# A two-layer graph network on 32 pairs: the column split, the product W a and the order of work rewritten

## The chip, the cores and the metric

One core of a Trainium2 chip runs the whole program. The metric is the device time of one execution in microseconds (us), lower is better; the median of the runs is compared. TensorE is the matmul engine (PE in the profile), DVE is VectorE, ACT is ScalarE, POOL is GpSimd, SP is the engine whose queue issues the transfers. PSUM is the memory that TensorE writes, eight banks of 128x512 f32; SBUF is the one that all engines read.

## The reference, cut to what matters

The input x is 64 batch entries of 128 nodes with 256 features, adj a 128x128 matrix of zeros and ones. Two residual layers follow one another.

```python
h = relu(layernorm(x))
# layer 0: graph attention with 4 heads, then one with 1 head, then an FFN
Wh = einsum('bnf,hfo->bhno', h, W)
f1, f2 = Wh @ a[:, :O], Wh @ a[:, O:]                  # per node and head
e = leaky(f1[..., :, None] + f2[..., None, :], 0.01)
attn = softmax(where(adj > 0, e, -1e9))
h2 = elu(attn @ Wh)                                    # heads side by side: 1024 features
out = elu(attention(h2, W_out, a_out))                 # the same with one head, 256 features
x = x + layernorm(relu(out @ w1 + b1) @ w2 + b2 + out) * gamma + beta
# layer 1
h3 = relu(layernorm(x))
x = x + deg * (h3 @ Wi.T + b) + adj @ (h3 @ Wj.T)
```

## The kernel before

Two batch entries form a pair; 32 pairs run through a pipeline of 8 stages. `steps` (L255) unrolls 39 steps on each engine. In step t, `pairs[k]` is pair t - k, if it exists, and each engine's function `one` lists the operations of all stages in one order, written out by hand; the same order is used in every step, and an engine goes strictly through it. What an operation needs it waits for with `wait` on a semaphore counter in `S`; `wait_bank` on TensorE waits until the last reader of a PSUM bank is done (which operation that is follows from the order). `B_...` (L41 to L60) gives each product its bank.

Precision: a factor is split into a high part in f32r (a copy by ACT, `..._hi`) and a low part (a subtraction by DVE or POOL, `..._lo`), and `three` (L1203) makes three products of them.

The path of a pair, with the names in the code:
- `norm1_stats`, `rstd1`, `norm1`: layer norm of x. `h_transposes` (L1269) and `ht_copy` give h transposed.
- `score_cols` (L1279): f1 and f2 of both entries as 16 columns, from h transposed times `wa` = W a (128 x C x 2 x H). `wa` is made once: DVE takes 16 dot products of rows of W with rows of a (`heads_dots` L523), for which each row of a_heads is loaded 128 times over (`ah_bc`, L273).
- The 16 columns must become rows that hold f2 exactly in bf16. `f_cols` (L601) writes them three times, at columns 32, 64 and 96 of a 128x128 tile `f_rep`; `score_rows` (L1291) transposes it in f32; `f_first` on ACT (L990) casts the rows to bf16, the first part; `f_less_first`, `f_second`, `f_third` (L587 to L599, through `less_first`, `second`, `third`) leave on DVE the second part in partitions 64 and up and the third in 96 and up. `scores` (L1297) multiplies them by the selector `rowsel`, which adds the three parts and repeats the row.
- `score_mask` (L643) adds f1 and the mask; `score_leaky`, `soft_max`, `soft_exp`, `soft_sum`, `soft` give the probabilities, `prob_transposes` (L1311), `at_high`, `at_low` their transposes.
- `gh_unit` (L1209) times u = 0..3 is h times attention, `gh_high` and `gh_low` split it; `h2_unit` (L1227), eight per pair, multiplies by W; `elu_exp`, `elu_less` (POOL), `elu` (DVE), `h2_high`, `h2_low` (POOL) make h2; `wh2_part` (L1250), eight per pair, multiplies by W_out, with W_out a_out as two more columns.
- The second attention has the same split on its 4 columns: `wh2_scores` (L665, once per entry), `score_rows2` (L1322), `g_first` to `g_third` (L617 to L630, on DVE), `scores2` (L1328), then `score_mask2` to `soft2`, `prob_transposes2`, `a2_copy`, `out2` (L1344).
- `out_exp`, `out_less`, `out_elu`, `ov_high`, `ov_low`; `hidden`, `hidden_relu`, `hidden_whole`, `hidden_low`; `ffn_out`, `ffn`, `add_b2`; `norm2_*`, `rstd2`, `norm2`, `scale2`, `add_beta`, `residual2`.
- `norm3_*`, `rstd3`, `norm3`, `h3_transposes` (L1387), `h3t_high`, `h3t_low`, `mixed` (L1397), `mj_high`, `mj_low`, `add_mi`, `gather` (L1412), `result`, `store`.

The transfers are issued on SP: x of the pair, then once the four parts of W and of a (L270), then W_out, a_out and the last weights (L275), w1 and w2 when the dots are done (L280), and in each step the residual's x and the store. Four constant rows are loaded by POOL's queue (L334). `out_dots` (L530) makes W_out a_out on DVE.

TensorE's order in a step before: scores 0, prob_transposes2, wh2 (0,0), out2, gh 0, scores 1, wh2 (1,1), gh 1, mixed 1, wh2 (1,2), gh 2, wh2 (0,1) (0,2), h_transposes, gh 3, wh2 (0,3) (1,3), score_cols, gather, hidden 0 and 1, score_rows2, h2 (0,0) (0,1), ffn_out, h2 (1,0), scores2, h3_transposes, score_rows, h2 (1,1), ffn 0 and 1, h2 (2,0), prob_transposes 0, h2 (2,1) (3,0) (3,1), wh2 (1,0), mixed 0, prob_transposes 1.

Of the kernel before, what the change touches and what calls it, by code (L numbers as in the profile page):

```python
# [21 lines left out]
BF16 = mybir.dt.bfloat16  # L22
# [14 lines left out]
G3 = (32, 64, 96)  # L37
# [3 lines left out]
B_HT = 5  # L41
B_COLS = 5
B_ROWS = 5
B_SCORES = (5, 4)
B_PROBS = (6, 6)
# [3 lines left out]
B_ROWS2 = 7  # L49
B_SCORES2 = 6  # L50
B_PROBS2 = 7
B_OUT = 7
B_HIDDEN = 6
B_FFN = 7
B_H3T = 4
B_M = (4, 6)
B_LAST = 4
B_ADJ = 2
B_L1W = (2, 3)


class Pair:
# [8 lines left out]
    def exists(self):  # L71
        return not isinstance(self.i, int) or 0 <= 2 * self.i + self.c < PAIRS

# [10 lines left out]
def build(nc, x, adj, w_heads, a_heads, w_out, a_out, w1, b1, w2, b2, gamma, beta, l1w, l1b, out):  # L84
    ctx = ExitStack()
    with ctx:
# [17 lines left out]
        rowsel = sb("rowsel", [P, 4 * H, P], BF16)  # L104
        sel = sb("sel", [P, 4 * H])
# [21 lines left out]
        ah_bc = lend2[:, 0:2, :, :, :].rearrange("p x y h m -> p (x y) (h m)")  # L127
# [27 lines left out]
        f_rep = two("f_rep", [P, P])  # L155
        f_parts = same("f_parts", [P, P], BF16)
        f_rest = same("f_rest", [P, P])
# [8 lines left out]
        f2_rep = two("f2_rep", [P, P])  # L166
        g_parts = two("g_parts", [P, P], BF16)
        g_rest = two("g_rest", [P, P])
# [23 lines left out]
        out_in, ffn_in, last_in = sem("out_in"), sem("ffn_in"), sem("last_in")  # L192
        adj_in, consts_in, memset_done, ident_ready = sem("adj_in"), sem("consts_in"), sem("memset_done"), sem("ident_ready")
# [6 lines left out]
        dotted = sem("dotted")  # L200
        w_hi_ready, w_lo_ready = sem("w_hi_ready"), sem("w_lo_ready")
# [6 lines left out]
        for per, names in (  # L208
# [5 lines left out]
                "rows_third"),  # L214
# [7 lines left out]
            (2, "wh2_done wh2_copied wh2_scores_copied exps2_done"),  # L222
            (1, "rows2_done rows2_first rows2_rest rows2_second rows2_third scores2_done "
# [41 lines left out]
        DOTS_HEADS, DOTS_ALL = 2 * C * H, 2 * C * H + 2 * K2  # L265
# [3 lines left out]
        def _(sp):  # L269
            def load_heads():  # L270
                for hd in range(H):
                    sp.dma_start(wh[:, :, hd, :], w_heads[hd].rearrange("(c f) o -> f c o", f=P)).then_inc(heads_in[hd], 16)
                    sp.dma_start(ah_bc[:, hd, :], a_heads[hd].partition_broadcast(P)).then_inc(heads_in[hd], 16)  # L273

            def load_later_weights():  # L275
                sp.dma_start(wo[:, :, :], w_out.rearrange("(k f) o -> f k o", f=P)).then_inc(out_in, 16)
                sp.dma_start(ao_bc[:, :, :], a_out.rearrange("(j o) -> j o", j=2).partition_broadcast(P)).then_inc(out_in, 16)
                sp.dma_start(l1w_sb[:, :, :], l1w.rearrange("(k o) d -> o k d", o=P)).then_inc(last_in, 16)

            def load_ffn_weights():  # L280
                sp.wait_ge(dotted, DOTS_HEADS)
# [21 lines left out]
            def one(pairs):  # L303
# [8 lines left out]
                if p := pairs[6]:  # L312
                    store(p)
                if p := pairs[2]:
                    load_residual(p)
# [6 lines left out]
        def _(pool):  # L322
# [11 lines left out]
            for dst, src in ((b2_bc, b2), (gamma_bc, gamma), (beta_bc, beta), (l1b_bc, l1b)):  # L334
                pool.dma_start(dst[:, :], src.partition_broadcast(P)).then_inc(consts_in, 16)
# [56 lines left out]
            def scale2(p):  # L392

                if p.is_first():
                    pool.wait_ge(consts_in, 80)
# [11 lines left out]
            def add_beta(p):  # L407

                if p.is_first():
                    pool.wait_ge(consts_in, 80)  # L410
# [29 lines left out]
            def one(pairs):  # L440
                if p := pairs[5]:
                    out_less(p)
                if p := pairs[4]:
                    h2_low(p, 3)
                if p := pairs[6]:
                    scale2(p)
                if p := pairs[5]:
                    ov_low(p)
                if p := pairs[2]:
                    h_low(p)  # L450
                if (p := pairs[3]) and p.is_first():
                    out_low()
                if (p := pairs[4]) and p.is_first():
                    ffn_low()
                if p := pairs[5]:
                    add_beta(p)
                if p := pairs[6]:
                    rstd3(p)
                if p := pairs[5]:
                    hidden_low(p)  # L460
                if p := pairs[3]:
                    elu_less(p, 0)
                if p := pairs[2]:
                    soft(p, 0)
                if (p := pairs[3]) and p.is_first():
                    out_scores_low()
                if p := pairs[3]:
                    elu_less(p, 1)
                if p := pairs[6]:
                    add_bias(p)  # L470
                if p := pairs[3]:
                    h2_low(p, 0)
                if p := pairs[2]:
                    soft(p, 1)
                if p := pairs[3]:
                    elu_less(p, 2)
                    elu_less(p, 3)
                    h2_low(p, 1)
# [4 lines left out]
                if p := pairs[0]:  # L483
                    rstd1(p)
# [4 lines left out]
        def _(dve):  # L489
# [11 lines left out]
            dve.memset(f_rep[0][:, :], 0.0)  # L501
            dve.memset(f_rep[1][:, :], 0.0)
            dve.memset(f2_rep[0][:, :], 0.0)
            dve.memset(f2_rep[1][:, :], 0.0)

            def selectors():

                dve.wait_ge(ident_ready, 1)
                dve.tensor_tensor(sel[:, :], ident[:, G3[0]:G3[0] + 4 * H], ident[:, G3[1]:G3[1] + 4 * H], ALU.add).then_inc(sel_ready, 1)
                dve.wait_ge(sel_ready, 1)  # L510
                dve.tensor_tensor(sel[:, :], sel[:, :], ident[:, G3[2]:G3[2] + 4 * H], ALU.add).then_inc(sel_ready, 1)
# [11 lines left out]
            def heads_dots(hd):  # L523
# [995 lines left out]
```

## Time and profile before

| what | value |
|---|---|
| runs | 907.23, 907.75, 909.05 us; median 907.75 |
| the profiled execution | 909.05 us, span of its instructions 907.2 us |
| TensorE (PE) busy | 836.8 us, 92% of the span |
| weight loads (PEld) | 776.6 us, 86%, beside the products |
| DVE, ACT, POOL busy | 757.1 (83%), 683.0 (75%), 703.9 us (78%) |
| mean granted TensorE clock | 0.989 |
| DMA | 31.5 MB, mean 35 GB/s, 246 GB/s in the first of 40 slices |

The span runs from the first to the last instruction. Products of TensorE overlap, so the distance from the start of one to the start of the next says more than its duration. "ps<-gh_hi,wh_hi" reads: written tile, and the tiles read. A time in brackets behind a row of the timeline is the idle time of that engine before it, with what ended it. The trace knows tiles by their memory, so `lend`, `wo`, `l1w_sb` and `h_hi` also stand for the tiles that share it or look alike.

### The profile page before, as it was taken

Reading aid. Unit: us, or ns where it says so; the run is one execution under the profiler, and the core shown is the slowest. Engines: PE = TensorE matmul, PEld = TensorE weight load, DVE = VectorE, ACT = ScalarE, POOL = GpSimd, SP = SyncE. Lnnn points to the kernel's source line nnn. Section 1 sums busy time; section 2 is a strip of 40 time slices with the busy share of each in tenths; the row PEclk is TensorE's granted clock in tenths of the full one; section 3 lists DMA queues with packets and bytes.
Section 4 is the critical chain, followed back from the end, with each engine's and each line's share of the span. In section 5 each row is a group of like instructions: output and inputs, shape, how many; then the busy total and the mean of one; then the engine's idle time right before and its main releaser. Section 6 shows DMA issues by size and latency. Waiting matters only on the chain.

```text
span 907.2 us, 20067 instructions
## 1 busy us (share of the span) xinstructions
PE 836.8 (92%) x6281; PEld 776.6 (86%) x6281; DVE 757.1 (83%) x1998; ACT 683.0 (75%) x1801; POOL 703.9 (78%) x948
## 2 busy tenths in 40 slices
PE   2699999999999999999999999999999999999964
PEld 1589989889998988999898899889889998989952
DVE  4978888898888889888888988888899888897753
ACT  3788878787777878778787877778777877877541
POOL 3587988877788887778888777888877788888852
PEclk9999999999999999999999999999999999999987
DMA  8100010111111011111101111110111111000000
GB/s 246 59 1 24 25 36 2 36 36 36 35 37 35 1 36 36 36 36 36 34 4 36 36 36 36 36 35 3 35 37 36 36 37 35 2 24 25 25 24 23
DMA packets 30136, 31.50 MB, mean 35 GB/s; under 512 B 1856, under 2 KB 28992, under 8 KB 30032
## 3 DMA queue, kind: packets, MB, share of 16 engines
q1 hardware_dynamic: 29776, 29.63, 10.5%
q8 instruction: 52, 0.85, 0.4%
q0 software_dynamic: 256, 0.59, 0.3%
q14 instruction: 52, 0.43, 0.2%
HBM read 21.82 MB, written 8.39 MB: 33 GB/s over the span
## 4 chain that ended last, share of the span: by engine, by line
PE 66%; DVE 17%; issue 9%; POOL 3%; ACT 2%; DMA 1%; SPq 0%; DVEq 0%; POOLq 0%; ACTq 0%
PE ps L1201 59%; DVE g_parts L598 4%; PE ps L1319 3%; DVE wo L711 2%; DVE lend L737 2%; PE ps L1275 2%; PE ps L1393 2%; DVE mj_lo L768 1%; DMA lend<-in_L_gnn_a_heads 1%; ACT mj_hi L1086 1%; DVE c_st L568 1%; DVE g_rest L589 1%; DVE g_parts L621 1%; DVE f_rep L669 1%; PE ps L1341 1%
## 5 line engine op out<-in xcount | busy, mean ns | idle before, releaser
L363 POOL TENSOR_TENSOR h_lo<-h2v,h_hi 128x512 fp32r<-128x512 f32 x128 | 166.6, 1302 | 0.1
L1201 PE MATMUL ps<-gh_hi,wh_hi 128*128 128x256 f32 x512 | 153.7, 300 | 1.6 <-DVE h2v L641 1.1
L1201 PE MATMUL ps<-wo_hi,h_hi 128*128 128x258 f32 x512 | 150.6, 294 | 0.0
L1201 PE MATMUL ps<-wo_lo,h_hi 128*128 128x258 f32 x512 | 145.1, 283 | 0.0
L1201 PE MATMUL ps<-wo_hi,h_lo 128*128 128x258 f32 x512 | 145.0, 283 | 0.0
L1201 PE MATMUL ps<-gh_lo,wh_hi 128*128 128x256 f32 x512 | 142.9, 279 | 0.0
L1201 PE MATMUL ps<-gh_hi,wh_lo 128*128 128x256 f32 x512 | 142.7, 279 | 0.0
L369 POOL TENSOR_SCALAR h2e<-h2e 128x512 f32<-128x512 f32 x128 | 86.2, 681 | 32.0 <-ACT h2e L959 31.8
L1201 PEld LDWEIGHTS ps<-wo_lo,h_hi 128*128 128x128 f32 x512 | 97.4, 190 | 4.3
L1201 PEld LDWEIGHTS ps<-wo_hi,h_hi 128*128 128x128 f32 x512 | 96.8, 189 | 4.6 <-POOL h_lo L363 0.4
L970 ACT ACTIVATE lend<-lend,zm 128x128 f32<-128x128 f32 x256 | 99.1, 393 | 0.0
L1201 PEld LDWEIGHTS ps<-gh_hi,wh_hi 128*128 128x128 f32 x512 | 96.5, 188 | 2.1 <-DVE h2v L641 1.5
L641 DVE SCALAR_TENSOR_TENSOR h2v<-h2e,ps 128x512 f32<-128x512 f32 x128 | 87.5, 683 | 12.9 <-POOL h2e L369 6.4
L582 DVE TENSOR_TENSOR gh_lo<-ps,gh_hi 128x512 fp32r<-128x512 f32 x128 | 87.7, 686 | 11.9 <-ACT gh_hi L948 11.9
L404 POOL TENSOR_TENSOR lend<-lend,zr 128x512 f32<-128x512 f32 x64 | 69.5, 1087 | 35.9 <-DVE zr L663 35.9
L1201 PEld LDWEIGHTS ps<-wo_hi,h_lo 128*128 128x128 f32 x512 | 97.0, 189 | 0.0
L1201 PEld LDWEIGHTS ps<-gh_hi,wh_lo 128*128 128x128 f32 x512 | 96.8, 189 | 0.0
L1201 PEld LDWEIGHTS ps<-gh_lo,wh_hi 128*128 128x128 f32 x512 | 96.7, 189 | 0.0
L948 ACT ACTIVATE gh_hi<-ps 128x512 fp32r<-128x512 f32 x128 | 75.8, 592 | 10.8 <-PE ps L1201 7.5
L1005 ACT ACTIVATE h_hi<-h2v 128x512 fp32r<-128x512 f32 x128 | 80.5, 629 | 0.3 <-DVE h2v L641 0.2
L959 ACT ACTIVATE h2e<-ps 128x512 f32<-128x512 f32 x128 | 72.1, 588 | 2.0 <-PE ps L1201 1.4
L413 POOL TENSOR_TENSOR wo<-xr,beta_bc 128x512 f32<-128x512 f32 x32 | 41.3, 1291 | 40.7 <-DVE lend L737 40.7
(166 smaller groups left out, 2794.3 us busy)
## 6 DMA issues: line engine op xcount, KB each, us to landing
xa<-in_x SPq DMA_DIRECT2D x32, 256.0 KB, 3.1
xr<-in_x SPq DMA_DIRECT2D x32, 256.0 KB, 3.0
out<-res SPq DMA_DIRECT2D x32, 256.0 KB, 2.2
lend<-in_L_gnn_W_heads SPq DMA_DIRECT2D x4, 256.0 KB, 5.7
lend<-in_L_gnn_a_heads SPq DMA_DIRECT2D x4, 256.0 KB, 8.4
wo<-in_L_gnn_W_out SPq DMA_DIRECT2D x1, 1024.0 KB, 11.2
l1w_sb<-in_L_gnn_W SPq DMA_DIRECT2D x1, 512.0 KB, 9.7
lend<-in_L_gnn_w SPq DMA_DIRECT2D x2, 256.0 KB, 3.0
```

The costliest lines, as they stand in the source:

```text
L363: pool.tensor_tensor(h2_lo[:, u, :, :].rearrange("p c n -> p (c n)"), h2v[u % 2][:, :], h2_hi[:, u, :, :].rearrange("p c n -> p (c n)").bi ...
L369: pool.tensor_scalar(h2e[u % 2][:, :], h2e[u % 2][:, :], 1.0, -1.0, ALU.mult, ALU.add).then_inc(S["heads_less"], 1)
L404: pool.tensor_tensor(zn[:, b, :, :], zp[:, b, :, :], zr[p.e][:, b, :].unsqueeze(2).broadcast_to([P, H, P]), ALU.mult).then_inc(S["probs_re ...
L413: pool.tensor_tensor(xb, xr[p.e][:, :, :], beta_bc[:, :].unsqueeze(1).broadcast_to([P, 2, F]), ALU.add).then_inc(S["x_plus_beta"], 1)
L582: dve.tensor_tensor(gh_lo[:, c, :, b, :], ps[:, B_GH[u], :].rearrange("p (h n) -> p h n", h=H), gh_hi[:, c, :, b, :].bitcast(F32), ALU.sub ...
L598: dve.tensor_tensor(parts[p.e][96:P, :], rest[p.e][96:P, :], parts[p.e][96:P, :], ALU.subtract)\
L641: dve.scalar_tensor_tensor(h2v[i][:, :], h2e[i][:, :], 0.0, ps[:, B_H2[u], :], ALU.min, ALU.max).then_inc(S["heads_elu"], 1)
L948: act.activation(gh_hi[:, c, :, b, :], ps[:, B_GH[u], :].rearrange("p (h n) -> p h n", h=H), ACT.Copy).then_inc(S["gh_hi"], 1)
L959: act.activation(h2e[u % 2][:, :], ps[:, B_H2[u], :], ACT.Exp).then_inc(S["heads_exp"], 1)
L970: act.activation(zp[:, b, hd, :], zt[:, b, hd, :], ACT.Exp, bias=zm[p.e][:, b, hd:hd + 1], accum_out=zs[p.e][:, b, hd:hd + 1]).then_inc(S[ ...
L1005: act.activation(h2_hi[:, u, :, :].rearrange("p c n -> p (c n)"), h2v[u % 2][:, :], ACT.Copy).then_inc(S["heads_hi"], 1)
L1201: return pe.matmul(out_, lhs, rhs, start=start, stop=stop)
```

## The change

**The split on columns.** The columns are split before they are turned into rows. `split_cols` on DVE copies the columns out of PSUM as f32 (for score_mask), casts them to bf16 as first part, subtracts that in PSUM itself, casts the rest as second part, and subtracts to the third. The three parts stand side by side at columns 0, 16 and 32 of a zeroed bf16 tile of 128x128 (`f_split`, `g_split`), which `score_rows` multiplies by the bf16 identity; one copy brings the rows to SBUF (ACT for f, DVE for g). `wh2_scores` now handles both entries at once.

**W a by TensorE.** The rows of a come as one 16x128 tile, are transposed once, each head's W is transposed by four transposes, copied by DVE, and multiplied in `heads_products`; the steps of these stand between the parts of pairs 0 and 1 in TensorE's order. The loads of a_heads for all partitions are gone. The four constant rows are loaded by SP, behind a_out and before the last weights.

**Identity products.** `warm(n, bank)` issues n products of the bf16 identity with itself, 128x512, into a bank that is not in use: 6 before the transposes of W, 2, 10, 3, 2 and 6 around the score steps of pairs 0 and 1, and at the end 10 before hidden of pair 31, 6 before h3_transposes of pair 30, 3 before its gather, and for pair 31 15, 4 and 3 before h3_transposes, mixed and gather.

**The orders** of all four engines, the banks and the wait_bank lists are new; store and load_residual change places on SP, and the stages are counted otherwise (store is in stage 7, load_residual in 3).

```diff
+            def split_cols(name, p, cols, whole, parts):
+                dve.tensor_copy(whole, cols).then_inc(S[name[0]], 1)
+                dve.tensor_copy(parts[0], cols).then_inc(S[name[1] + "_first"], 1)
+                wait(dve, name[0], p)
+                wait(dve, name[1] + "_first", p)
+                dve.tensor_tensor(cols, cols, parts[0], ALU.subtract).then_inc(S[name[1] + "_rest"], 1)
+                wait(dve, name[1] + "_rest", p)
+                dve.tensor_copy(parts[1], cols).then_inc(S[name[1] + "_second"], 1)
+                wait(dve, name[1] + "_second", p)
+                dve.tensor_tensor(parts[2], cols, parts[1], ALU.subtract).then_inc(S[name[1] + "_third"], 1)
...
             def score_rows(p):
-                wait(pe, "cols_copied", p)
-                pe.transpose(ps[:, B_ROWS, 0:P], f_rep[p.e][:, :], ident[:, :]).then_inc(S["rows_done"], 1)
+                wait(pe, "rows_third", p)
+                mm(ps[:, B_ROWS, 0:P], f_split[p.e][:, :], ident_bf[:, :], True, True).then_inc(S["rows_done"], 1)
...
+            def heads_transposes(hd):
+                pe.wait_ge(heads_in[hd], 16)
+                if hd >= 2:
+                    pe.wait_ge(wh_t_copied, hd - 1)
+                for k in range(C):
+                    for c in range(C):
+                        last = pe.transpose(ps[:, B_WHT[hd % 2], k * F + c * P:k * F + (c + 1) * P],
+                                            wh[:, c, hd, k * P:(k + 1) * P], ident[:, :])
+                last.then_inc(wh_t_done, 1)
+            def heads_products(hd):
+                pe.wait_ge(wh_t_copied, hd + 1)
+                pe.wait_ge(a_cols_ready, 1)
+                for c in range(C):
+                    for k in range(C):
+                        last = mm(ps[:, B_WA, 0:COLS].rearrange("p (c j h) -> p c j h", c=C, j=2)[:, c, :, hd],
+                                  wh_t[:, hd % 2, k * F + c * P:k * F + (c + 1) * P], a_cols[:, hd, :, k], k == 0, k == C - 1)
+                last.then_inc(wa_done, 1)
+            def warm(n, bank):
+                for _ in range(n):
+                    pe.matmul(ps[:, bank, :].rearrange("p (k n) -> p k n", k=4), ident_bf[:, :], ident_bf[:, :].unsqueeze(1).broadcast_to([P, 4, P]),
+                              start=True, stop=True)
```

TensorE's order in a step after (once-only parts in brackets): wh2 (1,2) (1,3), h2 (0,0) (0,1), [products 2], h2 (1,0), [products 3], h2 (1,1), score_cols, prob_transposes 0, hidden 0 and 1, score_rows2, h2 (2,0), score_rows, [a_transpose], scores2, [transposes 0 and 1], h2 (2,1) (3,0), ffn_out, [products 0], scores 0, h3_transposes, [transposes 2], h2 (3,1), wh2 (0,0), ffn 0 and 1, gh 0, mixed 0, [adj_transpose], prob_transposes2, mixed 1, wh2 (1,0), prob_transposes 1, out2, wh2 (0,1), [l1w_transposes], scores 1, gh 1, h_transposes, [transposes 3], wh2 (0,2), gather, [products 1], gh 2, wh2 (1,1), gh 3, wh2 (0,3).

DVE after: soft_max 1, norm3_stats, norm1, norm3_var, wh2_scores, elu 0, f_cols_split, rows2_copy, elu 1, soft_sum 1, hidden_whole, score_mask2, at_low 0, soft_max2, elu 2, h3t_low, soft_sum2, soft2, score_mask 0, add_b2, norm2, elu 3, add_mi 0, gh_low 0, mj_low 0 and 1, add_mi 1, soft_max 0, at_low 1, gh_low 1, score_mask 1, soft_sum 0, out_elu, gh_low 2, result, gh_low 3, residual2.

ACT after: wh2_copy 0 and 1, elu_exp 0, soft_exp 1, elu_exp 1, h2_high 0, hidden_relu, at_high 0, rows_copy, norm3, elu_exp 2, score_leaky2, h3t_high, [out_scores_high], h2_high 1, soft_exp2, elu_exp 3, [out_high], norm1, mj_high 0, a2_copy, h_high, h2_high 2, gh_high 0, score_leaky 0, mj_high 1, at_high 1, h2_high 3, out_exp, gh_high 1, soft_exp 0, gh_high 2, norm2, gh_high 3, score_leaky 1, ht_copy, ov_high.

POOL after: add_beta, elu_less 0, rstd1, elu_less 1, rstd3, h2_low 0, hidden_low, elu_less 2, h2_low 1, soft 1, elu_less 3, add_bias, [out_low], rstd2, h2_low 2 and 3, out_less, h_low, soft 0, scale2, ov_low.

## Rows read from the trace of the kernel before

**Rows 1.** Busy time of each engine in one steady period; columns: PE, PEld, DVE, ACT, POOL.
```profile
450.05:476.50 26.45, 25.58 (x198) 23.95 (x197) 23.22 (x61) 20.95 (x58) 21.56 (x29) 1.00 0.10 31
```

**Rows 2.** Waits: who waited for whom; total us, times, longest.
```profile
PE ps L1201 <- DVE g_parts L598: 25.4, 29, 1.2
```

**Rows 3.** Timeline of a steady period; start us, us, engine, line.
```profile
504.15 1.27 POOL L390 TENSOR_TENSOR hid_lo<-wo,hid_hi 128x512 fp32r<-128x512 f32 x1 [0.93 <-DVE wo L711]
504.22 1.36 DVE L598 TENSOR_TENSOR g_parts<-g_rest,g_parts 32x128 bf16<-32x128 f32 x1
...
504.49 0.28 PE L1201 MATMUL ps<-gh_hi,wh_lo 128*128 128x256 f32 x1
...
505.63 0.29 PE L1201 MATMUL ps<-g_parts,rowsel 128*128 128x128 bf16 x2 [0.87 <-DVE g_parts L598]
```

**Rows 4.** Groups of DVE instructions by line and form; busy us, mean ns.
```profile
L598 DVE TENSOR_TENSOR g_parts<-g_rest,g_parts 32x128 bf16<-32x128 f32 x32 | 39.2, 1224 | 1.0
...
L594 DVE CAST f_parts<-f_rest 64x128 bf16<-64x128 f32 x32 | 26.3, 822 | 1.0
...
L669 DVE COPY f_rep<-ps 128x6 f32<-128x6 f32 x64 | 9.8, 153 | 0.5 <-ACT l1w_sb L976 0.3
...
L598 DVE TENSOR_TENSOR f_parts<-f_rest,f_parts 32x128 bf16<-32x128 f32 x32 | 9.2, 289 | 1.0
...
L594 DVE CAST g_parts<-g_rest 64x128 bf16<-64x128 f32 x32 | 7.2, 224 | 1.1
```

**Rows 5.** Timeline of TensorE in stretches without a wait.
```profile
51.51 0.39 PE L1201 MATMUL ps<-f_parts,rowsel 128*128 128x128 bf16 x4
51.71 0.37 PE L1201 MATMUL ps<-wo_hi,h_hi 128*128 128x258 f32 x1
51.91 0.29 PE L1201 MATMUL ps<-wo_lo,h_hi 128*128 128x258 f32 x1
52.03 0.29 PE L1201 MATMUL ps<-wo_hi,h_lo 128*128 128x258 f32 x1
...
827.75 0.39 PE L1201 MATMUL ps<-l1w_hi,h_hi 128*128 128x512 f32 x1
827.98 0.40 PE L1201 MATMUL ps<-l1w_lo,h_hi 128*128 128x512 f32 x1
```

**Rows 6.** Groups by line and form on ACT and DVE, for the prices of chains.
```profile
L948 ACT ACTIVATE gh_hi<-ps 128x512 fp32r<-128x512 f32 x128 | 75.8, 592 | 10.8 <-PE ps L1201 7.5
...
L981 ACT ACTIVATE lend<-wo,b_nm,b_rs 128x256 f32<-128x256 f32 x64 | 34.6, 590 | 1.4 <-POOL b_nm L358 1.4
...
L582 DVE TENSOR_TENSOR gh_lo<-ps,gh_hi 128x512 fp32r<-128x512 f32 x128 | 87.7, 686 | 11.9 <-ACT gh_hi L948 11.9
```

**Rows 7.** The start: one row of the DMA issues, then the timeline.
```profile
lend<-in_L_gnn_W_heads SPq DMA_DIRECT2D x4, 256.0 KB, 5.7
...
14.24 0.42 DVE L499 SCALAR_TENSOR_TENSOR res<-lend 128x256 f32<-128x256 f32 x1 [2.88 <-DMA lend<-in_L_gnn_a_heads]
...
17.37 1.88 PE L1201 MATMUL ps<-wa,ht 128*128 128x8 f32 x8 [4.36 <-DVE res L499]
...
24.18 1.11 PE L1275 MATMUL ps<-ident,h 128*128 128x128 f32 x4 [1.75 <-ACT h L981]
...
40.20 0.66 PE L1275 MATMUL ps<-ident,h 128*128 128x128 f32 x4 [0.40 <-ACT h L981]
...
43.27 0.36 PE L1201 MATMUL ps<-gh_hi,wh_hi 128*128 128x256 f32 x1 [0.46 <-DVE gh_lo L582]
```

**Rows 8.** The end: timeline of TensorE; the first row is the last wh2 product.
```profile
859.82 0.28 PE L1201 MATMUL ps<-wo_hi,h_lo 128*128 128x258 f32 x1
...
894.19 1.11 PE L1393 MATMUL ps<-ident,lend 128*128 128x128 f32 x4 [3.89 <-ACT lend L981]
...
899.93 0.63 PE L1201 MATMUL ps<-l1w_lo,h_hi 128*128 128x512 f32 x1
900.36 0.63 PE L1201 MATMUL ps<-l1w_hi,h_lo 128*128 128x512 f32 x1
```

More of the change, by code:

```diff
@@ L441, in one @@
                 if p := pairs[5]:
[L442 to L455, printed above, removed]
-                    add_beta(p)
+                    add_beta(p)
+                if p := pairs[3]:
+                    elu_less(p, 0)
+                if p := pairs[0]:
+                    rstd1(p)
+                if p := pairs[3]:
+                    elu_less(p, 1)
                 if p := pairs[6]:
                     rstd3(p)
+                if p := pairs[3]:
+                    h2_low(p, 0)
                 if p := pairs[5]:
@@ L461, in one @@
                 if p := pairs[3]:
[L462 to L472, printed above, removed]
+                    elu_less(p, 2)
+                    h2_low(p, 1)
                 if p := pairs[2]:
@@ L482, in one @@
                     h2_low(p, 2)
-                if p := pairs[0]:
-                    rstd1(p)
+                    h2_low(p, 3)
+                if p := pairs[4]:
+                    out_less(p)
+                if p := pairs[1]:
+                    h_low(p)
+                    soft(p, 0)
+                if p := pairs[5]:
+                    scale2(p)
+                if (p := pairs[4]) and p.is_first():
+                    ffn_low()
+                if p := pairs[4]:
+                    ov_low(p)
             steps(one)
@@ L614, in f_third, with wh2_scores @@
-            def f_third(p):
-                third("rows", p, f_parts, f_rest)
-            def g_first(p):
+                split_cols(("cols_copied", "rows"), p, ps[:, B_COLS, 0:COLS], f_cols[p.e][:, :],
+                           [f_split[p.e][:, k * COLS:(k + 1) * COLS] for k in range(3)])
+            def wh2_scores(p):
+                wait(dve, "wh2_copied", p)
+                wait(dve, "rows2_done", p, lag=1)
+                split_cols(("wh2_scores_copied", "rows2"), p, ps[:, B_WH2[0]:B_WH2[0] + 2, F:WO], g_cols[p.e][:, :, :],
+                           [g_split[p.e][:, k * COLS:k * COLS + 4].rearrange("p (b j) -> p b j", b=2) for k in range(3)])
@@ new lines, in one @@
+                if p := pairs[2]:
+                    score_cols(p)
+                if p := pairs[3]:
+                    prob_transposes(p, 0)
+                if (p := pairs[6]) and p.number() == 31:
+                    warm(10, 0)
+                if p := pairs[6]:
+                    hidden(p, 0)
+                    hidden(p, 1)
+                if p := pairs[5]:
+                    score_rows2(p)
+                if p := pairs[4]:
+                    h2_unit(p, 2, 0)
+                if (p := pairs[2]) and p.number() == 0:
+                    warm(3, 0)
@@ L1482, in one @@
                 if p := pairs[4]:
+                    h2_unit(p, 3, 1)
+                    wh2_part(p, 0, 0)
+                if p := pairs[6]:
                     ffn(p, 0)
                     ffn(p, 1)
+                if p := pairs[3]:
+                    gh_unit(p, 0)
+                if (p := pairs[7]) and p.number() == 31:
+                    warm(4, 0)
+                if p := pairs[7]:
+                    mixed(p, 0)
+                if (p := pairs[1]) and p.is_first():
+                    adj_transpose()
```

669 lines of the change are left out of this document (337 added, 332 removed).

## The prediction

> **What bounds the kernel now.** I read the busy shares by engine first (the table above: TensorE 92%, more than any other), then one period of the steady part, then who waited for whom, and the two ends last. A pair of batch entries passes every 26.45 us; in such a period TensorE works 25.58 us, and DVE, ACT and POOL 23.2, 21.0 and 21.6 [rows 1]. So TensorE is the bound and idles 0.87 us per period. One wait makes up that idleness: 25.4 us in 29 times, always before the products that read g_parts [rows 2]. The timeline of one period shows how: the third part of the split (L598) starts at 504.22, just after POOL's subtraction L390 at 504.15, and lasts 1.36 us; TensorE's last product before it starts at 504.49, the next at 505.63 [rows 3]. The same line on f_parts takes 289 ns, on g_parts 1224 ns; L594 is 224 ns on g_parts and 822 on f_parts [rows 4]. The long ones end when a POOL instruction ends: two engines in each other's way. The Trainium skill (SBUF — State Buffer, Who interferes with whom) says that a DVE instruction with two SBUF inputs waits for a GpSimd instruction that reads SBUF, and that a PSUM input lifts this; the trace's 1224 ns agree. By it the changed split can't be held up, since none of its operations has two SBUF inputs.
>
> **Part 1, the split on columns.** Removed per pair: three small widening copies (two of them 153 ns), two subtractions, and the casts and third parts, 1224 + 289 + 822 + 224 ns [rows 4]: over 2.9 us of DVE. Added: two splits of five dependent operations on 128x16 and 128x4, and one copy of 128x128 on DVE that was there before under another name (g_first). The nearest row is the copy of 128x6 out of PSUM at 153 ns; with a hop to the next I take 5 x 0.18 = 0.9 us each. Upper end: one of the five is held by POOL as L598 was, 1.36 us, then 2.1; lower end 0.8. DVE loses about 1 us of work per period and is not the bound; ACT's copy of the rows stays as it was. On TensorE two f32 transposes of 128 columns (one start each 0.11 us) become bf16 products (0.05 each by the four in 0.20 us of [rows 5]); but behind those four the second product comes 0.20 us after the first and not 0.12, so I set the exchange at nothing, from -0.1 to +0.1 us per pair.
> What goes is the wait: **25.4 us**, unless another replaces it.
>
> **Part 2, the new orders.** The work on TensorE stays at 25.58 us per period, so I laid its new order out by starts of 0.12 us for 256 columns and 0.23 for 512 [rows 5]: six products 0.70, mixed 1.40, gh_unit 0.71, transposes of four 0.44, score_cols and out2 0.9 each. From the start of a period: score_cols ends at 5.2, rows2 is at 7.1, score_rows at 7.9, scores2 at 8.0, h3_transposes at 10.3, gh_unit 3 ends at 24.9. Then the chains that must fit:
> f_cols_split has from 5.4 to 7.9, needs 0.9, and DVE first ends elu 0 at 6.4: slack 0.6, gone if one of the five is held for 1.36.
> rows2_copy (about 0.29) has from 7.45 to 8.0: slack 0.25. Behind scores2 on TensorE everything would wait.
> elu 1 stands behind rows2_copy on DVE and ends at 8.45, its bank is wanted at 8.8: 0.3.
> h3_transposes wait for norm3 (1.1 us on ACT), which waits for rstd3 on POOL, behind ov_low, add_beta, two elu_less and rstd1. I get h3 ready at 10.15 against 10.3: slack 0.1.
> h2_unit 0 waits for the last gh_low. Between gh_unit 3 and it stood 4.4 us of products (two wh2 parts, score_cols, gather, hidden, rows2); now three wh2 parts, 2.16. Needed are 0.3 to end, 0.59 and 0.69 on ACT and DVE [rows 6], hops 0.15: 1.7. On ACT norm2 (two of 590 ns, [rows 6]) stands ahead of gh_high 3, so slack is 0.2.
> Four slacks under 0.3 us with steps known to 0.05: I take 0.1 us of new waiting per period, 3 us in 30, bounds 0 and 0.4 (12 us). Store and residual load change places on SP's queue; they carry 256 KB per pair that land in about 3 us, hidden. POOL loses four DMA issues at the start, where it waits anyway.
>
> **Part 3, the start.** The products of W a now wait for the broadcast rows of a: DVE's dots stood 2.88 us for them, and score_cols of pair 0 began at 17.37 [rows 7]. After: four loads of W alone. Issued from 1.7 at 0.45 us each, with half the bytes in the way, they should have landed by 9 (the median of W was 5.7 us from issue [rows 7]). TensorE then does four transposes and four f32 products per head: at 1.11 us per four transposes and 1.88 us per four f32 products, which the trace counts as eight [rows 7], 4 x 3.0 = 12 us. Its clock: four transposes took 1.11 us at 24.18 and 0.66 us at 40.20 [rows 7], so it ran at 1.2 GHz at the first and at 2.4 at the second, whatever the granted clock prints there; at 2.4 GHz the 12 us are some 6.5. Now TensorE works from about 3 us on (six products of the identity first). If it is at 2.4 GHz from about 11 us, W a is done at 14 and score_cols ends at 16, not at 19.3: 3.3 us gained. If it stays at 1.2 GHz, W a is done at 18.5 and score_cols at 21.5, 2.2 lost. From there the first h2_unit (43.27 [rows 7]) took 24 us, with out_dots on DVE in the middle. After, out_high, norm1 and h_high stand ahead of score_leaky on ACT and out_dots still ahead of the maximum, but scores waits for nothing else, and both soft steps come before out_low on POOL; the same walk gives 21. So h2 starts at 37 (fast clock) to 42 (slow); I take 38.5, gain 4.8. Of that 1.0 is not gained, as score_cols of pair 2 now comes after it. l1w is issued behind four more broadcasts, some 3 us later; TensorE waits for it with scores(0,1) and h_transposes(1) queued behind. Those are wanted about 5 us after scores(0,0), so that is hidden up to about 23 us.
>
> **Part 4, the end.** From the last wh2 product (its slot ends at 859.94) to 907.2 there are 47.3 us [rows 8]. Products at 1.2 GHz lie in it: in the last mixed ten of twelve start 0.43 us apart [rows 8] against 0.23: 2.0 us. The last h3_transposes take 1.11 [rows 8] against 0.66: 0.45. By the same ratio twelve products of the last ffn and eight of the last hidden lose 0.1 each, 2.0, and the gather before it 0.3. In all 4.7 at best. Also out2 should come about 0.8 earlier. The identity products fill gaps: 15 before the last h3_transposes take 3.5 us at 0.23 each in a gap of 3.9 [rows 8]; at 1.2 GHz they take 6.5 and delay it by 2.6. I take 4.5 of a possible 5.5, lower end 1.
> The Trainium skill (TensorE: Matmul & The Clock Gate, Part 4) states that transposes don't count as activity for the clock. The rows can't show it: no stretch has transposes alone. By it the start's 16 transposes would not help the clock, h2 would start at 42 and the sum would be 3.5 us higher; rival (b) has that case with a chance of its own.
>
> **The sum.** The profiled execution took 909.05 us, its span 907.2; the median of the runs is 907.75, 1.3 below. 909.05 - 25.4 + 3 - 4.8 + 1.0 - 4.5 = 878.35; against the median 877.
>
> **Rivals.** (a) A new wait takes the place of the old: at h3_transposes, scores2 or h2_unit 0, of 0.3 to 0.9 us per period. For it: slacks of 0.1 to 0.25. Against: back-to-back ACT steps overlap by about 0.1 us, which I left out. At 0.45 us: 877 - 3 + 13.5 = 887.5; at 0.9, 901. Chance 0.17.
> (b) The identity products don't lift the clock, so the change doesn't do what it says: the start at 42 (3.5 lost), the end gains 1 (3.5 lost): 884. For it: at the start transposes and waits surround them. Chance 0.15.
> (c) Slower: h2_unit 0 waits for gh_low 3, whose chain has lost 2.2 us of cover. If soft_exp and norm2 on ACT are late, everything behind h2_unit 0 moves, every period. It decides from about 1.1 us per period (32 us in 30); 2 us of lateness would give, less the 0.5 of cover, 1.5 x 30 = 45: 877 - 3 + 45 = 919. Against: ACT works 21.0 of 25.6 us. Chance 0.07.
> (d) The forecast: 868 to 884, chance 0.61.
>
> **The numbers.** Down to 867: no new wait (3), start at 37 (1.5), the end at its best (1.0), products shorter by 0.1 us per period (3) and a rest of 1.5 for idle spots that I left standing. Up to 889: (b), and (a) up to 0.5 us. A measurement of this kernel tells 0.2% from no change. Faster 0.91 (d, a, b, less what (a) leaves near none), same 0.02, slower 0.07.
>
> **What would show it.** Right: the period falls to 25.5 to 25.8 us; no DVE step of the two splits is over 0.3 us; the first wh_hi product of pair 0 starts before 41 us; the products of the last mixed start 0.23 us apart. Wrong: a line of TensorE in the waits with about 30 entries and over 6 us, above all behind gh_low, h3 or the g_parts copy; TensorE work per period far from 25.6.

## The result and the profile after

The kernel after takes 871.21 us (median of 4 runs, 869.2 to 872.8) against 908.16 for the kernel before beside it: a ratio of 0.9592, 95% interval 0.9567 to 0.9617. The forecast was 877, the range 867 to 889. The profiled execution took 870.21 us with a span of 868.3; against 907.2 that is 38.9 us to account for.

The page's busy shares:

```profile
PE 849.3 (98%) x6400; PEld 785.6 (90%) x6400; DVE 701.7 (81%) x2002; ACT 668.0 (77%) x1801; POOL 693.6 (80%) x944
```

One period of the steady part, start to start of the products that read g_parts, answers to [rows 1] (columns: busy us of PE, PEld, DVE, ACT, POOL, then the granted clock, DMA share, GB/s):

```profile
460.03:485.41 25.38, 25.38 (x198) 23.97 (x198) 21.30 (x62) 20.48 (x57) 21.32 (x30) 1.00 0.10 28
```

TensorE is busy in every one of the 25.38 us. The period was 26.45, so it fell by 1.07, and only 0.87 of that was idle time: the busy time for the same number of TensorE instructions (198) also fell by 0.20 us, from the 25.58 of before. Half of that belongs to the wait too, as rest_psum shows below. These are all the waits of TensorE of at least 0.5 us in total (total us, times, longest), to be read against [rows 2]:

```profile
PE ps L1414 <- ACT lend L968: 3.3, 2, 2.3
PE ps L1210 <- POOL ident_bf L343: 2.8, 1, 2.8
PE ps L1222 <- ACT ht L974: 2.5, 1, 2.5
PE ps L1222 <- DVE gh_lo L601: 1.6, 1, 1.6
PE ps L1222 <- POOL ov_lo L397: 1.5, 2, 1.3
PE ps L1414 <- DVE l1w_sb L675: 1.1, 1, 1.1
PE ps L1222 <- ACT f_parts L980: 0.8, 2, 0.5
PE ps L1222 <- DVE h_lo L759: 0.5, 1, 0.5
PE ps L1222 <- DVE mj_lo L765: 0.5, 2, 0.3
PE ps L1222 <- DVE g_parts L635: 0.5, 1, 0.5
```

None comes more than twice: all lie at the two ends, the one behind g_parts too (at 828.98). Nothing took the place of the 29 waits behind g_parts. The groups of the split on DVE (busy us, mean ns), against [rows 4]:

```profile
L612 DVE TENSOR_TENSOR ps<-ps,f_split 128x16 f32<-128x16 f32 x32 | 5.9, 183 | 3.3
L614 DVE CAST f_split<-ps 128x16 bf16<-128x16 f32 x32 | 5.6, 174 | 1.1
L616 DVE TENSOR_TENSOR f_split<-ps,f_split 128x16 bf16<-128x16 f32 x32 | 5.6, 174 | 1.1
```

and one of them in full (ns min/median/max, first and last start us):

```profile
L612 DVE TENSOR_TENSOR ps<-ps,f_split x32: 182/183/183, 17.8 to 762.5; 128x16 f32<-128x16 f32 x32
```

No step was ever held: 182 to 183 ns over all 32 pairs, where L598 had a mean of 1224.

The start and the end on TensorE's timeline, against [rows 7, 8]; the first row is the first product of wh_hi of pair 0 (43.27 before), the others belong to the end:

```profile
40.27 0.36 PE L1222 MATMUL ps<-gh_hi,wh_hi 128*128 128x256 f32 x1 [1.63 <-DVE gh_lo L601]
...
852.52 3.41 PE L1210 MATMUL ps<-ident_bf 128*128 128x512 bf16 x15
858.19 0.66 PE L1414 MATMUL ps<-ident,lend 128*128 128x128 f32 x4 [2.26 <-ACT lend L968]
...
860.60 0.40 PE L1222 MATMUL ps<-l1w_lo,h_hi 128*128 128x512 f32 x1
860.83 0.39 PE L1222 MATMUL ps<-l1w_hi,h_lo 128*128 128x512 f32 x1
```

The last four transposes take 0.66 us in place of 1.11, the last products start 0.23 us apart in place of 0.43, and the fifteen products of the identity end 2.26 us ahead of the next real work, so they delay none. With the last wh2 product at 826.31 (its slot of 0.12 us ends at 826.43), the account of the 38.9 us is:

| stretch | before, us | after, us | gain |
|---|---|---|---|
| span's start to the first wh_hi product of pair 0 | 43.27 | 40.27 | 3.0 |
| from there to the end of the last wh2 product | 816.67 | 786.16 | 30.5 |
| from there to the end of the span | 47.3 | 41.9 | 5.4 |

### The profile page after: what moved, and what is told of

Read it like the earlier page. It is cut to its first block, busy times and chain, and to the rows that moved or that the text cites. A ratio compares the mean times of both kernels' runs of the same rounds, so it can differ in the third digit from the quotient of the medians.

```text
span 868.3 us, 20346 instructions
## 1 busy us (share of the span) xinstructions
PE 849.3 (98%) x6400; PEld 785.6 (90%) x6400; DVE 701.7 (81%) x2002; ACT 668.0 (77%) x1801; POOL 693.6 (80%) x944
## 4 chain that ended last, share of the span: by engine, by line
PE 94%; POOL 2%; DVE 1%; ACT 1%; issue 1%; POOLq 0%; ACTq 0%; DVEq 0%
PE ps L1222 84%; PE ps L1340 4%; PE ps L1414 2%; PE ps L1296 2%; PE ps L1395 2%; PE ps L1362 1%; PE ps L1210 1%; ACT lend L968 0%; ACT lend L957 0%; PE ps L1181 0%; DVE res L510 0%; POOL wo L425 0%; POOL lend L409 0%; POOL h_lo L375 0%; DVE lend L734 0%
## 5 line engine op out<-in xcount | busy, mean ns | idle before, releaser
L946 ACT ACTIVATE h2e<-ps 128x512 f32<-128x512 f32 x128 | 75.6, 591 | 32.7 <-PE ps L1222 32.7
L416 POOL TENSOR_TENSOR lend<-lend,zr 128x512 f32<-128x512 f32 x64 | 71.8, 1123 | 23.9 <-DVE zr L668 23.9
L381 POOL TENSOR_SCALAR h2e<-h2e 128x512 f32<-128x512 f32 x128 | 79.8, 623 | 10.1 <-ACT h2e L946 9.9
L656 DVE SCALAR_TENSOR_TENSOR lend<-ps,f_cols,mask_bf 128x128 f32<-128x128 f32 x256 | 71.4, 339 | 0.8 <-PE ps L1222 0.8
```

The costliest lines, as they stand in the source:

```text
L381: pool.tensor_scalar(h2e[u % 2][:, :], h2e[u % 2][:, :], 1.0, -1.0, ALU.mult, ALU.add).then_inc(S["heads_less"], 1)
L416: pool.tensor_tensor(zn[:, b, :, :], zp[:, b, :, :], zr[p.e][:, b, :].unsqueeze(2).broadcast_to([P, H, P]), ALU.mult).then_inc(S["probs_re ...
L656: last = dve.scalar_tensor_tensor(zt[:, b, hd, :], ps[:, B_SCORES[b], hd * P:(hd + 1) * P], f_cols[p.e][:, f1:f1 + 1], mask_bf[:, :], ALU. ...
L946: act.activation(h2e[u % 2][:, :], ps[:, B_H2[u], :], ACT.Exp).then_inc(S["heads_exp"], 1)
```

## The experiments

Twelve runs followed in three lots, each beside runs of the kernel before. All medians in one place; the period is the median one of the profiled execution, where before has 26.45, and the last column is that of the same single execution:

| run | us, median | ratio to before, 95% | period, us | first wh_hi product, us |
|---|---|---|---|---|
| rest_psum | 882.47 | 0.9714 (0.9692 to 0.9736) | 25.48 | 43.40 |
| third_up | 884.52 | 0.9733 (0.9719 to 0.9748) | 25.52 | 43.07 |
| split_only | 898.10 | 0.9879 (0.9861 to 0.9898) | 25.92 | 42.00 |
| no_warm | 878.66 | 0.9666 (0.9652 to 0.9680) | 25.38 | 43.91 |
| rest_sbuf | 874.06 | 0.9623 (0.9607 to 0.9638) | 25.37 | 39.73 |
| dots_back | 867.81 | 0.9553 (0.9539 to 0.9568) | 25.22 | 42.93 |
| warm_end | 874.34 | 0.9622 (0.9609 to 0.9635) | 25.38 | 43.58 |
| late_dots | 874.91 | 0.9637 (0.9616 to 0.9658) | 25.38 | 41.03 |
| after_again | 871.10 | 0.9584 (0.9565 to 0.9602) | 25.38 | 41.91 |
| placed | 867.44 | 0.9541 (0.9519 to 0.9564) | 25.22 | 43.77 |
| pad64 | 871.91 | 0.9585 (0.9570 to 0.9601) | 25.38 | 42.20 |
| early_start | 871.62 | 0.9586 (0.9563 to 0.9608) | 25.22 | 42.83 |

### Is it the collision? rest_psum and third_up

Both start from the kernel before and keep its split of 128 columns. The first puts the rests in PSUM:

```diff
-dve.tensor_tensor(rest[p.e][64:P, :], psum[64:P, :], parts[p.e][64:P, :], ALU.subtract)
+dve.tensor_tensor(rest[64:P, :], psum[64:P, :], parts[p.e][64:P, :], ALU.subtract)
-g_parts, g_rest)
+g_parts, ps[:, B_WH2[0], 384:512])
```

> The kernel before with the rests of both splits written to PSUM and not to SBUF, nothing moved and nothing else changed, so that the second and third part read at most one operand from SBUF. Theory (DVE and POOL are in each other's way at SBUF): the third part of g falls from 1224 to about 290 ns, the cast of f from 822 to about 230, TensorE's 25.4 us of waiting behind g_parts go, the period is 25.6 us, the time about 908 - 25 = 883. Rival (the third part is late because DVE comes to it late): its duration falls little or the wait stays, the time is over 900.

The second moves one call:

```diff
 g_less_first(p)
 g_second(p)
+g_third(p)
...
-if p := pairs[5]:
-    g_third(p)
```

> The kernel before with the third part of g moved up on DVE, right behind the second part; operands stay in SBUF. In the trace POOL is idle there (about 502.96 to 504.15 of the steady period). Theory: the third part takes 290 ns there, the wait goes, time about 883, so that the stall was a matter of place too; the cast of f keeps its 822 ns. Rival: the port is held at any place, or hidden_whole now comes later and POOL's hidden_low with it: 890 or more.

In rest_psum the same two lines (groups on DVE, mean ns) are no longer held:

```profile
L598 DVE TENSOR_TENSOR g_parts<-ps,g_parts 32x128 bf16<-32x128 f32 x32 | 9.5, 297 | 1.0
L594 DVE CAST f_parts<-ps 64x128 bf16<-64x128 f32 x32 | 9.4, 294 | 1.0
```

The same run shows that the wait cost more than its idle time. In [rows 3] the product at 504.49 is followed by the one on g_parts at 505.63, 1.14 us later; here it is 0.16:

```profile
464.24 0.28 PE L1201 MATMUL ps<-gh_hi,wh_lo 128*128 128x256 f32 x1
464.40 0.29 PE L1201 MATMUL ps<-g_parts,rowsel 128*128 128x128 bf16 x2
```

So the wait took 0.98 us of a period and showed 0.87 as idle: a product of 0.28 us is overlapped by the next one where nothing waits, and that overlap was lost as well. With the instructions, orders and tiles of before but without the wait, the period is 25.48, not 25.58.

In third_up the operands stay in SBUF, the third part merely begins before GpSimd's subtraction hid_lo (at 463.50 in a steady period, hid_lo at 464.77):

```profile
L594 DVE CAST f_parts<-f_rest 64x128 bf16<-64x128 f32 x32 | 21.2, 662 | 1.0
L598 DVE TENSOR_TENSOR g_parts<-g_rest,g_parts 32x128 bf16<-32x128 f32 x32 | 9.2, 289 | 1.1
```

Either takes the 25.4 us of waiting away (1.1 us in two waits are left in rest_psum) and with it 24 to 26 us of the time. So the wait was the collision at one place of the period; two thirds of the whole gain needs neither the column split nor the new orders, and one moved line is enough for it. The cast on f_parts, still held at 662 ns in third_up, costs nothing in the middle, since no engine waits for it there. That cast has one SBUF input: the prediction had named two inputs only. The Trainium skill (SBUF — State Buffer, Who interferes with whom) lists copies and casts, where their operands meet its conditions, among what can take the pair of ports shared with GpSimd. The trace agrees: 822 and 662 ns on average from SBUF against 294 from PSUM.

### The column split without the new orders: split_only

The kernel before with `split_cols` in place of the old split, put where the copies f_cols and wh2_scores stood, all other orders as they were.

> The kernel before with the column split alone (both splits, bf16 products for the rows), in the old orders, without W a by TensorE and without identity products. Theory: the wait of 25.4 us goes, and TensorE's work per period falls by up to 0.2 us if the f32 transposes were dearer than the bf16 products: 877 to 883. Rival: the five dependent steps of g hold up score_rows2 in the old order by about 0.3 us per period: 890.

The wait behind g_parts is gone, yet 10.5 of 37 us is all it brings. The waits show what came instead:

```profile
PE ps L1355 <- ACT lend L944: 12.2, 32, 3.9
```

h3_transposes now wait for norm3 in every pair, and the period is 25.92. Half of the 12.2 us are the last three pairs (0.6, 1.5 and 3.9); in the middle it is 0.22 us in each. There too a wait costs more than its idle time: from the start of the product before to the start of the first transpose it is 0.43 us, where it is 0.06 in the kernel before. These 0.37 are most of the 0.44 by which the period is above that of rest_psum. Neither expectation had the place right: score_rows2 does not wait, h3_transposes do. That place is one of the prediction's rival (a), and in these orders it is real. So the column split needs the new orders, which keep h3 in time: the wait is absent from the middle after. The split was not needed for the gain in the middle, though: rest_psum had most of it in the old orders, and no_warm below, with the column split, the new orders and W a on TensorE, is 3.8 us faster than rest_psum.

### What the identity products are worth: no_warm and warm_end

no_warm issues none; warm_end keeps those of pairs 30 and 31 at the end.

```diff
-for _ in range(n):
+for _ in range(0):
     pe.matmul(ps[:, bank, :]...
```

> The changed kernel without any of the identity products, all else the same. Theory: steady part unchanged (period 25.4), products at 1.2 GHz come back at the end as before (some 4 us) and the start is 0 to 3 us later: 875 to 878 against 871. Rival: the identity products gain nothing, since they stand in waits that others end: 871 within 1 us.

> The kernel after with the identity products at the end alone (the 27 at the start left out). They fill gaps, so they are worth time by the clock alone. If the 7.5 us that all of them were worth is 3.6 at the start and 3.8 at the end, as the two profiles put it, this is 874.5 to 875.5 us with the first product of wh_hi at 43.5 to 44 and 41.9 us from the last product of wh2 to the end. If the start's products are worth nothing because a later wait absorbs the start, it is 871 to 872 us.

Without them the time is 878.66, with the end's alone 874.34, with all 871.1: 4.3 us at the end, 3.2 at the start; the runs with and without do not overlap in either case. They only fill idle time, so this is the clock's part. In no_warm the end shows it in the waits: what was 3.3 us behind lend is 7.5.

```profile
PE ps L1414 <- ACT lend L968: 7.5, 2, 5.7
```

That run also answers another question: W a on TensorE without them starts the first wh_hi product at 43.91, no earlier than the 43.27 of before, in one profile of each.

### Does W a belong on TensorE? dots_back

W a by sixteen dot products of VectorE again, a_heads loaded as broadcasts, everything else as after.

> The kernel after, with W a made by sixteen dot products of VectorE again (the vector a loaded as four broadcasts), identity products kept where they are. If W a on TensorE is worth time, the first product of wh_hi of pair 0 starts later than 40.3 by the 3 us or more that the dot products stand on VectorE ahead of score_cols of pair 0: 43 or later, 874 to 877 us. If W a on TensorE brings nothing by itself (the run without identity products had its first such product at 43.9, later than the 43.3 of the kernel before), it starts at 40 to 41 and the time is 870 to 872 us. Nothing after the first product of wh_hi changes: period 25.4, end 41.9 us after the last product of wh2.

The first wh_hi product moved back to 42.93, as the first theory had it, and yet the time fell, to 867.81. The steady period fell as well, to 25.22 us, although its instructions are those of the kernel after. Groups of TensorE by form over the same 500 us, first after, then dots_back (mean ns in the last column but one):

```profile
L1222 PE MATMUL ps<-gh_hi,wh_lo 128*128 128x256 f32 x320 | 90.2, 282 | 0.0
...
L1222 PE MATMUL ps<-w_hi,hid_hi 128*128 128x256 f32 x80 | 22.5, 281 | 0.0
```

```profile
L1179 PE MATMUL ps<-gh_hi,wh_lo 128*128 128x256 f32 x320 | 89.4, 279 | 0.0
...
L1179 PE MATMUL ps<-w_hi,hid_hi 128*128 128x256 f32 x80 | 22.1, 276 | 0.0
```

Three ns less for the one kind of product and five for the other; not every kind changed. What differs beside the start is where the tiles lie: a_rows and a_cols take 576 bytes of each partition, and all tiles allocated behind them lie that much higher.

### The place of the tiles: placed, pad64, after_again

```diff
-a_rows = sb("a_rows", [COLS, P])
-a_cols = sb("a_cols", [P, H, 2, C])
...
 res = two("res", [P, 2, F])
+a_rows = sb("a_rows", [COLS, P])
+a_cols = sb("a_cols", [P, H, 2, C])
```

pad64 adds 64 bytes in the old place; after_again is the kernel after.

> The kernel after, unchanged, so that it is timed on the same chip as the three beside it. The first four runs of it had a median of 871.2 us (869.2 to 872.8); 870 to 872 us is expected, with a period of 25.38 us.

> The kernel after with the two tiles that the change adds for a_heads (a_rows, a_cols: 576 bytes of each partition) allocated behind all the others, so that every later tile lies 576 bytes lower, where it lay in the run dots_back. Not one instruction differs. In dots_back the period of a pair was 25.22 us against 25.38 in the kernel after, and the products of gh with wh_lo took 279 ns on average against 282, those of w_hi with hid 276 against 281. If the place of the tiles is the cause, the period is 25.22 here too, the first product of wh_hi stays at 40.3, and the time is 4 to 5 us shorter than after_again (0.16 us by some 29 periods): 866 to 867 us. If the cause is something else that dots_back left out, nothing changes: within 0.5 us of after_again.

> The run placed with 64 bytes of padding where the two tiles were: every later tile lies 64 bytes higher than in placed and 512 bytes lower than in the kernel after. If only the address within 512 bytes matters, the period is that of the kernel after, 25.38 us, and the time that of after_again within 0.5 us. If nothing of the place matters, all three are equal. If the place matters in some other way, the period lies at neither 25.22 nor 25.38.

The copies of g_parts on DVE mark the period; in placed:

```profile
460.53 0.29 DVE L635 CAST g_parts<-ps 128x128 bf16<-128x128 f32 x1 [0.79 <-PE ps L1222]
485.75 0.29 DVE L635 CAST g_parts<-ps 128x128 bf16<-128x128 f32 x1 [0.79 <-PE ps L1222]
```

and in pad64:

```profile
461.32 0.29 DVE L636 CAST g_parts<-ps 128x128 bf16<-128x128 f32 x1 [0.81 <-PE ps L1223]
486.70 0.29 DVE L636 CAST g_parts<-ps 128x128 bf16<-128x128 f32 x1 [0.81 <-PE ps L1223]
```

25.22 against 25.38, and 867.44 against 871.91 us. Between these two the means of some products differ (gh_hi with wh_hi 295 against 298 ns, w_hi with hid_hi 276 against 281), those of others hardly do (wo_hi with h_hi 293 against 294), and one goes the other way (mj_lo with adj_t 398 against 392). Shown: not one instruction differs between placed and the kernel after, 64 bytes of shift bring the longer period back, and 512 bytes between pad64 and the kernel after do nothing. From the first wh_hi product to the end of the last wh2 product it is 786.16 us in both profiles of the kernel after and 781.6 in placed. So placed, which has a shorter median than both kernels, is the version to keep. Which operand's address matters, and why, these runs do not tell.

dots_back has the tiles where placed has them and takes 867.81 against 867.44. So W a on TensorE is worth nothing that can be measured here, though the two were timed in different lots.

### How much cover the split has: rest_sbuf

```diff
-dve.tensor_tensor(cols, cols, parts[0], ALU.subtract)
+dve.tensor_tensor(rest, whole, parts[0], ALU.subtract)
```

with the rests in SBUF tiles of 16 and 4 columns.

> The kernel after, except that the rests of both splits go to small SBUF tiles of 16 and 4 columns again, so that two of the five steps read two SBUF inputs beside GpSimd's work. If it is the collision with GpSimd on SBUF that made a step long, some steps of this split show a mean of 250 to 500 ns in place of 164 to 183 ns. If the period was freed by the shorter steps (168 ns each, whatever holds them), the time becomes more than 1% longer (over 880 us). My theory is that the columns' split stands so far ahead of its reader in the new orders that a held step is covered: 871 to 874 us, period 25.4 to 25.5, no wait of TensorE behind g_split or f_split of over 0.3 us on average.

```profile
L613 DVE TENSOR_TENSOR f_rest<-f_cols,f_split 128x16 f32<-128x16 f32 x32 | 16.2, 506 | 3.3
L613 DVE TENSOR_TENSOR g_rest<-g_cols,g_split 128x4 f32<-128x4 f32 x32 | 15.1, 472 | 3.3
```

The collision is back: 506 ns for 16 columns and 472 for 4, against 183 and 171. The period stays, at 25.37: in the middle the new orders cover the held steps. The time is 3 us longer all the same. It goes where the pipeline fills (from the first wh_hi product to the end of the last wh2 product the profile has 3.3 us more than that of the kernel after); the row product of f_split is late there:

```profile
64.92 0.22 PE L1223 MATMUL ps<-ident_bf,f_split 128*128 128x128 bf16 x1 [1.30 <-DVE f_split L617]
```

with another 1.4 us behind the same line between 38 and 60 us. My theory had the period right and the total too low.

### Two tries at the start: late_dots and early_start

late_dots moves the dot products of W_out behind others on VectorE, with group 3 ahead of gh_low 2 and 3 of pair 0, and GpSimd's wo_lo ahead of h_low(0). early_start is placed, with group 2 behind score_mask(0,1) and group 3 ahead of gh_low 0.

> The kernel after with the eight dot products that stand on VectorE between score_mask(0,0) and soft_max(0,0) moved into its later gaps, and GpSimd's low part of W_out moved from 32.6 to before h_low(0) (20.9 to 25.1). In the profile of the kernel after they hold soft_max(0,0) until 24.82 while its input is there by 22.9. If that chain sets the start, the first product of wh_hi of pair 0 starts 1.5 to 2.5 us earlier (38 to 39 against 40.27) and the time is 869 to 870 us. If the start is set by other waits (GpSimd's h_low, the clock at 1.2 GHz from 28 to 35), it starts at 39.8 or later and the time stays within 0.5 us of 871.2.

> The run placed with another order at the start: of the dot products for W_out, group 2 moves from ahead of soft_max(0,0) to behind score_mask(0,1), group 3 to ahead of gh_low 0 of pair 0; GpSimd's low part of W_out moves ahead of h_low(0). In late_dots the same idea brought the last gh product of pair 0 from 38.6 to 37.4, but group 3 then stood ahead of gh_low 3, TensorE waited 3.54 us for it and ran at 1.2 GHz afterwards. Here no dots stand there. My theory: first product of wh_hi of pair 0 at 37.5 to 39, clock at 2.4 GHz behind it, 1.5 to 2.5 us below placed: 864 to 865.5 us. If the start is given back later (the fill is bound by another engine), it equals placed within 0.5 us; if a held dot product or the clock takes it, it is slower than placed.

Both fell. In late_dots the gh products ended at 37.4, as hoped, but group 3 held gh_low:

```profile
41.03 0.36 PE L1222 MATMUL ps<-gh_hi,wh_hi 128*128 128x256 f32 x1 [3.54 <-DVE gh_lo L601]
...
42.76 0.42 PE L1222 MATMUL ps<-gh_lo,wh_hi 128*128 128x256 f32 x1
42.98 0.42 PE L1222 MATMUL ps<-gh_hi,wh_lo 128*128 128x256 f32 x1
```

and behind that wait products start 0.22 us apart in place of 0.12: the lower clock. The profiled execution is 2.3 us longer than that of after_again: it starts 0.9 earlier, loses 1.6 in the middle and 1.6 at the end, and the last is not explained. In early_start one dot product of the four beside GpSimd's subtraction was held until that subtraction had ended (ns min/median/max, then GpSimd's own):

```profile
L510 DVE SCALAR_TENSOR_TENSOR res<-wo,oe x4: 415/944/4390, 19.8 to 25.9; 128x256 f32<-128x256 f32 x4
```

```profile
L353 POOL TENSOR_TENSOR wo_lo<-wo,wo_hi x1: 4466/4466/4466, 19.8 to 19.8; 128x2048 fp32r<-128x2048 f32 x1
```

That put soft_max(0,0) 7.5 us behind the start of score_mask(0,0) (26.20 against 18.74), where placed has 4.9. By the medians early_start is 4.2 us slower than placed. That the held dot product took these 4.2 us is likely but not shown: the profiled executions are the fastest of the one (869.1) and the slowest of the other (870.0), and in them the first wh_hi product comes at 42.83 and 43.77. Whether the dots alone, moved without GpSimd's low part, gain anything wasn't tried.

## Why the prediction was right, and where it was off

The main mechanism held: the 25.4 us of waiting went whole, by the step named, and the five steps of a split take 0.95 us (f) and 0.90 us (g) from the first start to the last end, where 0.9 was taken. The forecast was 6 us too high against the median. By its own steps, the profiled execution being 8.1 us below the sum of 878.35:

- **New waits, taken as 3 us, were 0.** The wait list after has no line in the middle. The four slacks of 0.1 to 0.3 us all held. The range held it as its lower bound. That the danger was real split_only shows: the wait of h3_transposes cost 0.37 us there in each pair.
- **Work of TensorE per period, taken as unchanged at 25.58 us, was 25.38.** Over some 30 periods that is 6 us, twice the "3" that the range allowed for. Half of it is a mis-sized wait: the prediction took the idle time of 0.87 us as all that the wait behind g_parts cost, while by starts it cost 0.98, so that without it the same work takes 25.48 (rest_psum). For the other half, the prediction treated the cadence of a product as a property of its shape. The runs show it also hangs on where the tiles lie: 0.16 us per period for 64 bytes. How much of the remaining 0.10 is place, how much the two f32 transposes turned into bf16 products, and how much the new neighbours of each product (those of mj_hi with adj_t fell from 480 to 395 ns, those of ov_hi with w_hi rose from 282 to 301) isn't settled.
- **Middle as a whole:** 25.4 + 6 - 1.0 for score_cols of pair 2 = 30.4, against 30.5 in the table.
- **Start, taken as 4.8 (first wh_hi product at 38.5), was 3.0 in the first profile and 1.4 in the second** (41.91). Of the same kernel, then, one start differs from another by 1.6 us, and placed, with the same instructions, has 43.77. The durations show where: eight transposes of W and the last 24 small products of W a took 1.07 and 3.91 us in the one and 1.95 and 5.12 in the other,

```profile
8.76 1.07 PE L1181 MATMUL ps<-ident,lend 128*128 128x128 f32 x8
9.66 3.91 PE L1222 MATMUL ps<-a_cols,lend 128*128 128x2 f32 x24
```

```profile
9.68 1.95 PE L1181 MATMUL ps<-ident,lend 128*128 128x128 f32 x8
11.42 5.12 PE L1222 MATMUL ps<-a_cols,lend 128*128 128x2 f32 x24
```

  so TensorE reached 2.4 GHz before them in the first only. Of the seven profiles that have both W a on TensorE and its identity products, these transposes took 1.07 to 1.40 us in four and 1.95 in three; without the identity products of the start (no_warm, warm_end) 1.95 in both. The step that failed is "at 2.4 GHz from about 11 us": even in the first profile, where W a was done at 13.4 (forecast: 14), it fell back to 1.2 GHz (a granted clock of 0.50 from 12 to 20 us), and score_cols of pair 0 took 1.85 us as before and that of pair 1 1.74 after another gap, where 0.95 is the price at 2.4 GHz (43.19 in the first profile). Score_cols of pair 0 ended at 17.2 in place of 16, and from there to the first wh_hi product it took 23.0 us where the walk had 21. The gain that the start does have comes from the identity products (3.2 us), not from W a on TensorE (nothing measurable).
- **End, taken as 4.5, was 5.4**; 5.5 had been put as the most possible. 4.3 of it is the identity products', by no_warm and warm_end.

Sum of the errors against the profiled execution: 3 + 6 - 1.8 + 0.9 = 8.1. The errors of the two unpriced terms have one sign, those of the ends nearly cancel.

Rival (a) did not come about in the new orders and did in the old ones. Rival (b) fell: 7.5 us are the identity products'. The sentence of the Trainium skill (TensorE: Matmul & The Clock Gate, Part 4) that transposes don't count for the clock was not put to a test of its own by any of the runs. Rival (c) fell: the only wait behind gh_low is the 1.6 us of pair 0.

Of "what would show it": the split's steps below 0.3 us, the first product before 41 (in one profile of two) and the 0.23 us at the end came true; the period came out at 25.38, below the 25.5 to 25.8 given.

## What to carry to other kernels

When one wait repeats once per period, look first at the instruction that it ends on: if its mean is several times that of the same line on other data, another engine may hold it, and moving that one call or its operand out of SBUF may give most of what a rewrite gives. Price a wait by the distance between the starts of the two products around it, not by the idle time alone. When the engine that sets the bound no longer waits, its time per period still isn't fixed: allocate tiles that are used once behind those of the loop, and compare the period of two placements before trusting a difference of half a per cent. Judge a start by more than one profile, and look which VectorE instructions a long GpSimd instruction will lie over before moving it.

## What the runs showed of the hardware

- A wait of TensorE costs the overlap of its products as well as the idle time: 0.87 us of idle time took 0.98 us by starts (before against rest_psum), 0.22 took 0.37 (split_only against before).
- Some of the same products on the same data took 3 to 5 ns more, of some 280, when the tiles lay 64 bytes higher (pad64 against placed), and no more than that when they lay 512 bytes higher again (the kernel after): 0.16 us in 25.4 of TensorE's period.
- A dot product of VectorE on two SBUF tiles of 256 columns, 0.41 us alone, took 4.39 beside a GpSimd subtraction of 4.47; a subtraction of 4 columns took 472 ns on average in place of 171. In these cases a held instruction's price followed the other's rest and not its own size.
- Behind the wait of 3.54 us in late_dots TensorE's products of 256 columns ran 0.21 us apart from 42.4 to 45.1, the rate of 1.2 GHz (a granted clock of 0.52), although TensorE was busy throughout; such a price of a wait stands in no line of the waits.
